# Edge messages of a two-layer graph network: the scalar-by-edge-vector product formed before the C weights are applied, and the weights read from PSUM

## The reference, cut to what matters

```python
h = SILU_NORM * silu(edge_scalars @ (W_fc1 / 8.0))
weight = h @ (W_fc2 / 8.0)                       # 4 * 32 weights of an edge: wA, wC, wD, wB
g0 = f0[edge_src]                                # 32 scalars of the source node
g1 = f1[edge_src]                                # 32 vectors of the source node
e0, e1 = edge_attr[:, :1], edge_attr[:, 1:]      # a scalar and a vector of the edge
outA = wA * g0 * e0
outB = wB * einsum('euk,ek->eu', g1, e1) / SQRT3
outC = (wC * g0)[..., None] * e1[:, None, :]
outD = wD[..., None] * g1 * e0[..., None]
# each is summed over the edges that end in a node (edge_dst), then multiplied by small matrices
```

## Time and profile before

| | us |
|---|---|
| median of 3 runs (8849.36 to 8855.67) | 8852.3 |
| the profiled execution, its own time | 8858.68 |
| span of its trace | 8856.9 |
| DVE busy in the whole span | 5237.0 (59%) |
| PE busy in the whole span | 7666.6 (87%) |
| POOL busy in the whole span | 3591.5 (41%) |

### The profile page before, as it was taken

How to read it: one execution, slowest core, us unless ns; L and a number is a source line. 1 busy time by engine, 2 the same in 40 slices (tenths; PEclk the granted TensorE clock), 3 DMA queues, 4 the chain that set the end, 5 groups by cost and what they waited for, 6 DMA issues and landing times. The chain is left out here.

```text
span 8856.9 us, 128455 instructions
## 1 busy us (share of the span) xinstructions
PE 7666.6 (87%) x37616; PEld 5771.0 (65%) x37617; DVE 5237.0 (59%) x12795; ACT 4088.0 (46%) x7196; POOL 3591.5 (41%) x3586
## 2 busy tenths in 40 slices
PE   1799999988999979999878888888888888888884
PEld 1333333336888858888767777777777777777774
DVE  4899999984333343333365555555555555555556
ACT  1577777765666646666542222222222222222224
POOL 6100002000000010000057777777777777777774
PEclk9999999998999989999987778777777877787876
DMA  1244443445555545555452322223232323322223
GB/s 31 62 100 93 93 100 73 105 93 166 143 143 143 143 134 142 142 143 143 128 147 78 79 78 78 79 78 79 78 79 78 79 78 79 79 78 79 78 75 99
DMA packets 630136, 880.48 MB, mean 99 GB/s; under 512 B 199533, under 2 KB 516940, under 8 KB 623456
## 3 DMA queue, kind: packets, MB, share of 16 engines
q1 hardware_dynamic: 500478, 495.87, 20.5%
q0 software_dynamic: 116640, 374.64, 17.7%
q10 hardware_dynamic: 12738, 6.40, 0.3%
HBM read 681.29 MB, written 195.26 MB: 99 GB/s over the span
## 5 line engine op out<-in xcount | busy, mean ns | idle before, releaser
L1451 POOL DMA_INDIRECT t_rows<-table,t_ends x3224 | 3182.7, 987 | 1009.3 <-issue 967.6
L893 ACT ACTIVATE c_wide_act<-c_raw 128x1000 fp32r<-128x1000 uint8 x1400 | 1454.1, 1041 | 693.0 <-PE c_sums L963 693.0
L945 DVE CAST c_wide_dve<-c_raw 128x1000 fp32r<-128x1000 uint8 x1400 | 769.0, 551 | 1381.0 <-PE c_sums L963 1380.9
L963 PE MATMUL c_sums<-c_wide_act,c_parts 128*128 128x500 f32 x5600 | 1504.6, 391 | 72.8 <-DVE c_parts L929 66.0
L1552 PEld LDWEIGHTS t_sums<-t_hot,t_msg_ad 128*128 128x128 f32 x6464 | 945.0, 230 | 935.7 <-issue 935.6
L1552 PE MATMUL t_sums<-t_hot,t_msg_ad 128*128 x6464 | 985.3, 318 | 639.6 <-DVE t_hot L1639 634.8
L633 DVE TENSOR_SCALAR a_key_hot<-a_key_tab,key_t 128x490 bf16<-128x490 f16 x5000 | 1469.5, 549 | 0.0
L677 ACT ACTIVATE a_a_sb<-a_sums 128x980 bf16<-128x980 f32 x1250 | 1246.1, 997 | 448.8 <-PE a_sums L660 426.9
L1605 DVE TENSOR_TENSOR t_ge<-t_rows,t_attrs 128x768 f32<-128x768 f32 x403 | 386.4, 959 | 1702.0 <-DMA t_rows<-table,t_ends 1558.0
L660 PE MATMUL a_sums<-a_key_hot,a_lo_hot 128*128 128x490 bf16 x5000 | 1310.9, 374 | 9.3 <-DVE a_key_hot L633 9.3
L1463 ACT ACTIVATE t_scal_t<-t_turned 128x512 f32<-128x512 f32 x403 | 240.7, 597 | 2303.2 <-PE t_turned L1511 2303.2
(11 more groups left out here) (201 smaller groups left out, 6118.4 us busy)
## 6 DMA issues: line engine op xcount, KB each, us to landing
c_raw<-a_dram SPq DMA_DIRECT2D x700, 437.5 KB, 3.5
a_dram<-a_a_sb POOLq DMA_DIRECT2D x50, 3062.5 KB, 17.8
t_scal<-in_edge_attr SPq DMA_DIRECT2D x403, 256.0 KB
t_rows<-table,t_ends POOLq DMA_INDIRECT x3224
t_ends<-in_edges SPq DMA_DIRECT2D x403, 8.0 KB
t_attrs<-in_edge_attr SPq DMA_DIRECT2D x403, 16.0 KB
table<-n_out SPq DMA_DIRECT2D x24, 256.0 KB, 2.3
n_xin<-in_x SPq DMA_DIRECT2D x24, 256.0 KB, 3.4
```

The costliest lines, as they stand in the source:

```text
L893: act.activation(to, of, ACT.Copy).then_inc(act_wide, 1)
L945: dve.tensor_copy(to, of).then_inc(dve_wide, 1)
L963: mm = pe.matmul(sums[s % 2][:], parts[:, part, h], wide[unit % 2][:, due % USLOTS, j], start=h == 0 and part == 0, stop=h == HI - 1 and p ...
L1451: pool.indirect_dma_start(out=rows[:, slot, t, :], out_offset=None, in_=table, in_offset=bass.IndirectOffsetOnAxis(ap=ends[:, slot, t:t + ...
```

## The change

The product of g0 and e1 is made in SBUF, as `g0e`, with 768 elements at each partition, right after `ge`. `cg` is no longer made. The C messages are then the product of the C weights, read from the PSUM tile `weight`, and `g0e`. `chain_sem` is still raised four times a group. Nothing else is changed; no other engine's instructions are touched.

```diff
-        cg = sb("cg", [P, T, MUL])
+        g0e = sb("g0e", [P, T, 3, MUL])
...
                     dve.tensor_tensor(ge[:], g1, e1[:, :, :, None].to_broadcast(wide), ALU.mult
                                       ).then_inc(chain_sem, 1)
 
+                    dve.tensor_tensor(g0e[:], g0[:, :, None, :].to_broadcast(wide),
+                                      e1[:, :, :, None].to_broadcast(wide), ALU.mult).then_inc(chain_sem, 1)
+
                     dve.wait_ge(ad_ready, g + 1)
-                    dve.tensor_tensor(cg[:], w[:, :, 2 * MUL:3 * MUL], g0, ALU.mult).then_inc(chain_sem, 1)
                     dve.tensor_tensor(msg_ad[:, b, :, MUL:D].rearrange("p t (k u) -> p t k u", k=3),
                                       ad[:, b, :, None, MUL:2 * MUL].to_broadcast(wide), g1, ALU.mult)
...
                     dve.tensor_tensor(msg_bc[:, b, :, MUL:D].rearrange("p t (k u) -> p t k u", k=3),
-                                      cg[:, :, None, :].to_broadcast(wide),
-                                      e1[:, :, :, None].to_broadcast(wide), ALU.mult)
+                                      w[:, :, None, 2 * MUL:3 * MUL].to_broadcast(wide), g0e[:], ALU.mult)
                     dve.wait_ge(chain_sem, base + 4)
```

## The result

The changed kernel takes 9038.4 us (median of 4 runs, 9034.9 to 9042.7) against 8852.1 us before: a ratio of 1.021, 95% interval 1.0193 to 1.0228, 186 us slower. The prediction was 9034 us in a range of 9000 to 9085. The profiled execution took 9040.9 us, its span is 9038.9.

The account below looks back on a forecast made before the run. POOL's back-to-back gathers were taken as the bound. 183 us of holds under the D messages, less 2 for other groups, plus 0.5 at the end, made +182 us: 9034 us, range 9000 to 9085.

Parts of the forecast that it names:

- What bounds the kernel: In `product_edges`, POOL issues 3224 gathers back to back and they set the pace, not PE or DVE.
- The hold under the D messages: The gather at 2.08 us starts 0.34 into the later D messages and is held 0.476 us: 183 us over 385 groups.
- DVE's 0.53 us in itself worth nothing: DVE's 0.53 us more a group is hidden by its 4.25 us idle ahead of L1605; uncovered, 214 us.
- The price of the PSUM read: C messages reading PSUM stay 0.95 us; rival: dearer read makes the hot matrix hold a gather, +12 to +50 us, chance 0.04.
- The A messages back to 0.42: L1612, which took 0.46 us with a gather starting beside it, would take 0.42 after the change.
- The gather let go between L1605 and `g0e`: The gather held by L1605 goes on at 0.834, before `g0e` starts at 0.876, at no new cost.
- the rival of 9185 us: L1605 and `g0e`, back to back, hold the gather as one, to 1.70 us: +333 us, chance 0.07.
- Landing times: They move the gather's start inside L1605 and may shift by 0.04 us on average: 15 us to either side.
- The other 18 groups: Groups mostly without the L1605 hold: `g0e` holds a gather 0.57 us, L1619 no longer holds one 0.68: -2 us.
- The range: Holds of 166 to 204 us and landing shifts give 9000 to 9055 us; with dearer PSUM reads up to 9084.
- the raster: Per-group times of DVE instructions and gather starts; a gather inside a two-SBUF-input instruction waits until about 0.13 us before its end.

Follow-up runs that it names:

- e2: The changed kernel with `g0e` made from the C weights in PSUM and the edge vectors (one SBUF input, same length): 9022.9 us.
- g3: The changed kernel with SP's loads of a later group issued when a group's rows have landed, not when it is done: 8922.3 us.
- g1: The kernel before with SP's loads of a later group issued when a group's rows have landed, DVE order unchanged: 8992.7 us.
- f2: The change's arithmetic with scaled A and D weights in PSUM and DVE order D messages, `g0e`, A messages, ge, dot, C, B: 8888.7 us.
- r1: The changed kernel repeated unchanged, five rounds beside the kernel before: 9026.8 us, ratio 1.0199.
- e1: The changed kernel with the scaled A and D weights left in the PSUM tile in place of `ad` in SBUF: 9050.9 us.
- e3: The changed kernel with the A messages before the D messages, nothing else: 9054.2 us.
- f1: The kernel before with scaled A and D weights in PSUM and DVE order D messages, ge, cg, A messages, dot, C, B: 8795.1 us.
- f3: The same instructions as f1 in DVE order cg, A messages, ge, D messages, dot, C, B: 8836.4 us.
- g2: As g1, with DVE order ge, cg, A, dot, D, B, C and `ad` in SBUF as before: 8702.4 us.

## Why the prediction was right, and where its sum was luck

- **What bounds the kernel**: right. POOL's gathers are the stage, in all 13 profiles.
- **The hold under the D messages**: forecast 385 x 0.476 = 183 us; measured 388 gathers, 189 us, held 0.488 each (median). This term is the result. e2 shows that it is the place of the D messages and not `g0e`'s own inputs.
- **DVE's 0.53 us in itself worth nothing**: right; g3 against g1 and f2 against the change show it from two sides.
- **The price of the PSUM read**: none. The C messages take 0.947 before and 0.946 after (medians over 403), and the one-hot matrix's hold stayed 0.17 us clear as forecast (one-hot 5.58 behind ge, gather at 6.32).
- **The A messages back to 0.42 (they had 0.46), idle time ahead of L1605 still 4.3 us, issue gaps unchanged**: right.
- **The gather let go between L1605 and `g0e`**: right; the rival of 9185 us rested on it. The gathers held by L1605 were held 0.36 in the median, none on through `g0e`.
- **Landing times**: I put them at nothing in the sum and gave 15 us to either side; L1605's holds grew by 8 us in the first profile after and shrank by 2 in r1's.
- **The total**: closer than the working deserves. The first to last gather grew by 199 us where the terms gave 182, and the missing 17 us were given back by the earlier stage that happened to end 18 us sooner in that execution (first gather at 4503.0, not 4521.4). In r1 the stretch grew by 184 us. The 199 us are 189 under the D messages, 8 more under L1605, 9 under `g0e` less 9 that L1619 no longer holds, 3 us of small holds gone, and some 4 us by which the plain gathers were longer in that execution (0.9453 in place of 0.9437).
- **The other 18 groups**: the sum had 17 x 0.57 gained and 17 x 0.68 given back; 15 gathers were held by `g0e`, for 9 us, and 13 were freed of L1619, 9 us. They cancel, as forecast.
- **The range**: its own terms, 204 us of holds and 15 for landing, reach to some 9070 us and not to 9055. The measured time lies far from that end, so nothing hung on it.
- In the expectations behind the prediction, the term that failed in e1, e3, f1, f2 and f3 was the landing time, taken as 3.24 us or near it whatever DVE did; and the 0.09 to 0.17 us that a gather adds to L1632 was not in the raster at all.

## What to carry to other kernels

Where GpSimd issues indirect DMAs back to back and sets the pace, don't judge a VectorE edit by VectorE's load: look at which VectorE instruction lies over each gather's start. Instructions with a PSUM input or one input belong there, those with two SBUF inputs between the starts; and since the pattern locks to the moment when the data lands, a load that delays the last gather belongs to the same raster. An edit of either sign may only be a change of phase, so test it in a second phase before you keep it or throw it away.

## What the runs showed of the hardware that I had not expected

- A gather holds DVE too, but only in its last part. `rel` (128x8, int32 to float32, one SBUF input) takes 0.22 us when it starts 0.1 to 0.2 us into a gather (389 times in the trace before). Where it starts 0.5 to 0.7 into one it ends with the gather: 0.31 in e1 (374 times), 0.39 in e3 (367 times). Instructions with two SBUF inputs that start just behind a gather's start aren't held: the A messages after a released gather took their plain 0.42 in the earlier trace rows and in all of the trace after. The Trainium skill, "SBUF — State Buffer", section "SBUF: two separate sides", says that whichever of the two engines starts first keeps the shared ports for its whole instruction, against a VectorE instruction in a two-port mode or, if the GpSimd one reads SBUF, with two SBUF inputs. The rows agree with "whole instruction" neither for those A messages nor for a `rel` that starts early in a gather; whether `rel` runs in such a mode no run shows.
- The landing time of a gather, from its start, was 2.60 us with no 256 KB load near it (g1, g2, g3, median) and 3.24 to 3.5 with one issued 0.3 to 0.5 us behind it. That the load's bytes stand ahead of the gather's in the DMA queues is my reading; no run took the queues apart, nor the 256 KB load from the small ones.
- A TENSOR_TENSOR of 768 float32 elements takes 0.946 us with one input broadcast out of PSUM (the change, median of 403) and 0.947 with both in SBUF (the C messages before).
